# A gated block with a mixture of experts: when the second expert's down weights are loaded, and in which order the last step takes its chunks

## The reference, cut to what matters

```python
logits = x @ gate_w.T; scores = softmax(logits); topk_w, topk_idx = top_k(scores, 2)
buf = zeros((16, 256, 512)).at[sorted_e, pos].set(x[sorted_t])     # up to 256 tokens per expert
g = silu(buf @ w_gate[e]); u = buf @ w_up[e]                       # 512 -> 352
expert_out = (g * u) @ w_down[e]                                   # 352 -> 512
y = (gathered expert rows * topk_w).sum over the two experts
sh = (silu(x @ ws_gate) * (x @ ws_up)) @ ws_down                   # shared, 512 -> 704 -> 512
x = x + tanh(g_ffn) * (y + sh)                                     # x in the layer is normalised
```

## Time and profile before

| | before |
|---|---|
| median of 3 runs | 579.65 us (579.65 to 580.83) |
| profiled execution, its own time | 581.87 us |
| its span | 579.8 us |
| mean granted clock of TensorE | 0.985 |
| PE busy | 546.2 us (94%) |
| DVE busy | 419.4 us (72%) |
| ACT busy | 331.0 us (57%) |
| POOL busy | 154.3 us (27%) |
| moved between HBM and the core | 89.52 MB in all |

### The profile page before, as it was taken

The page is one execution under the profiler, slowest core; times in us unless marked ns, Lnnn a source line. Parts: engine busy times, 40 slices in busy tenths (PEclk is TensorE's granted clock), DMA queues, the critical chain, the costliest instruction groups (busy, mean ns, idle before and its releaser), DMA issues.

```text
span 579.8 us, 10175 instructions
## 1 busy us (share of the span) xinstructions
PE 546.2 (94%) x3768; PEld 464.0 (80%) x3776; DVE 419.4 (72%) x828; ACT 331.0 (57%) x570; POOL 154.3 (27%) x187
## 2 busy tenths in 40 slices
PE   7897879999999999999799999999999999999995
PEld 3453548986888788887799999999999999999983
DVE  3778988998899786586376666766676776566766
ACT  3285876686558527522367677766666666742321
POOL 3437780431043010104022211111111100166610
PEclk9988999999999999999899999999999999999998
DMA  7930130014001130115757776666777767457742
GB/s 265 386 131 2 37 136 11 2 37 145 1 5 35 73 101 1 77 46 165 244 165 263 246 252 222 222 222 227 242 244 260 245 218 241 148 167 214 232 147 99
DMA packets 45891, 89.52 MB, mean 154 GB/s; under 512 B 4304, under 2 KB 24784, under 8 KB 44832
## 3 DMA queue, kind: packets, MB, share of 16 engines
q1 hardware_dynamic: 40736, 72.26, 36.7%
q0 software_dynamic: 5120, 16.78, 9.3%
HBM read 72.25 MB, written 16.78 MB: 154 GB/s over the span
## 4 chain that ended last, share of the span: by engine, by line
PE 62%; DVE 19%; ACT 6%; POOL 6%; issue 4%; DMA 2%; another core or an unknown queue 1%; SPq 0%; DVEq 0%; POOLq 0%; ACTq 0%
PE ps_gu L1854 10%; PE ps_gu L1855 10%; PE ps_gu L1856 10%; PE ps_d L1854 6%; PE ps_d L1856 5%; PE ps_d L1855 5%; PE ps_a L2108 3%; PE ps_gu L1896 2%; POOL w L486 2%; DMA raw_d<-in_L_ffn_w_down 2%; PE ps_gu L2415 2%; POOL sw_lo L502 1%; PE ps_d L1875 1%; DVE bn_b L1093 1%; ACT y L754 1%
## 5 line engine op out<-in xcount | busy, mean ns | idle before, releaser
L1854 PE MATMUL ps_gu<-ex_xhi,w_hi 128*128 128x256 f32 x352 | 99.4, 283 | 0.2 <-DVE ex_xlo L1469 0.2
L1855 PE MATMUL ps_gu<-ex_xlo,w_hi 128*128 128x256 f32 x352 | 99.5, 283 | 0.0
L1856 PE MATMUL ps_gu<-ex_xhi,w_lo 128*128 128x256 f32 x352 | 99.4, 282 | 0.0
L1854 PEld LDWEIGHTS ps_gu<-ex_xhi,w_hi 128*128 128x128 f32 x352 | 67.0, 190 | 2.5 <-DVE ex_xlo L1469 0.5
L1855 PEld LDWEIGHTS ps_gu<-ex_xlo,w_hi 128*128 128x128 f32 x352 | 67.1, 191 | 1.8
L1856 PEld LDWEIGHTS ps_gu<-ex_xhi,w_lo 128*128 128x128 f32 x352 | 67.1, 191 | 0.0
L1854 PE MATMUL ps_gu<-xt_hi,sw_hi 128*128 128x256 f32 x220 | 65.1, 296 | 0.1
L996 ACT ACTIVATE ex_hhi<-ex_hid 128x256 fp32r<-128x256 f32 (+1 forms) x66 | 27.5, 417 | 64.6 <-DVE ex_hid L1715 58.0
L1855 PE MATMUL ps_gu<-xt_lo,sw_hi 128*128 128x256 f32 x220 | 62.0, 282 | 0.0
L1856 PE MATMUL ps_gu<-xt_hi,sw_lo 128*128 128x256 f32 x220 | 62.0, 282 | 0.0
L1854 PE MATMUL ps_d<-wd_hi,ex_hhi 128*128 128x512 f32 x132 | 54.3, 411 | 6.6 <-DVE ex_hlo L1717 6.5
(11 more groups left out here) (255 smaller groups left out, 1411.4 us busy)
## 6 DMA issues: line engine op xcount, KB each, us to landing
raw_gu<-in_L_ffn_w_gate SPq DMA_DIRECT2D x16, 704.0 KB
raw_gu<-in_L_ffn_w_up SPq DMA_DIRECT2D x16, 704.0 KB
raw_d<-in_L_ffn_w_down SPq DMA_DIRECT2D x16, 512.0 KB
expert_out_scratch<-eo SPq DMA_DIRECT2D x16, 512.0 KB
w<-in_fside_BxS2xS SPq DMA_DIRECT2D x4, 1024.0 KB, 5.4
x2n_scratch<-y SPq DMA_DIRECT2D x4, 1024.0 KB, 3.9
x<-in_x SPq DMA_DIRECT2D x1, 3072.0 KB, 16.5
raw_d<-in_L_ffn_w_down SPq DMA_DIRECT2D x16, 192.0 KB
```

The lines of the kernel that those rows point to most:

```text
L1854: pe.matmul(dst, a_hi, b_hi, start=start, stop=False)
L1855: pe.matmul(dst, a_hi, b_lo, start=False, stop=False)
L1856: return pe.matmul(dst, a_lo, b_hi, start=False, stop=stop)
```

## The change

There are three edits. SP loads expert 1's gate and up first, waits for them (32), and then issues the two down transfers; `weights_gu(1)` on ACT waits for 32, and `weights_d(1)` gets a wait for 64. In the last step the chunks are taken in the order 0, 2, 1 (`part_at`), on PE, ACT and DVE alike. On DVE, `add_rows` and `add_last` stand one slot of `hidden` earlier, and `last_rows` adds the first bank after a count of its own (`first_half_done`, raised by the third of the last six products) and the second after all of them.

```diff
+    def part_at(e, m):
+        return (0, 2, 1)[m] if e == NE - 1 else m
...
             sp.wait_ge(sh_gu, CHUNKS)
-            load_raw(1, 1)
+            load_gu(1, wg_v[1], wu_v[1])
+            sp.wait_ge(raw_in[1], 32)
+            load_d(1, w_down[1])
...
             def weights_gu(e, k, q):
-                act.wait_ge(raw_in[q], 32 if isinstance(e, int) and e == 0 else 64 * k + 64)
+                act.wait_ge(raw_in[q], 32 if isinstance(e, int) and e < 2 else 64 * k + 64)
...
             def weights_d(e, q):
+                if isinstance(e, int) and e < 2:
+                    act.wait_ge(raw_in[q], 64)
                 if isinstance(e, int) and e == 0:
-                    act.wait_ge(raw_in[q], 64)
                     emptied_b(act, unit_b(B - 1, B_LGT))
...
-            def hidden(e, q, m, first):
-                n, k = M * e + m, ROWS[m]
+            def hidden(e, q, m, first, part=None):
+                part = m if part is None else part
+                n, k = M * e + m, ROWS[part]
...
                 if not first:
-                    act.wait_ge(ex_d, n - M + 1)
-                act.activation(ex_hhi[0:k, m, :], ex_hid[0:k, (q + m) % 2, :], ACT.Copy).then_inc(ex_hi, 1)
+                    act.wait_ge(ex_d, n - m + part - M + 1)
+                act.activation(ex_hhi[0:k, part, :], ex_hid[0:k, (q + m) % 2, :], ACT.Copy).then_inc(ex_hi, 1)
...
             def last_rows():
-                dve.wait_ge(ex_d, M * NE)
                 dve.wait_ge(sum_last, HALF)
                 for k in range(HALF):
                     j = HALF * h + k
+                    if k == 0:
+                        dve.wait_ge(first_half_done, 1)
+                    else:
+                        dve.wait_ge(ex_d, M * NE)
...
             shared_rows(1)
-            hidden(E + 4, 0, 1)
             dve.wait_ge(ex_eo, E + 1)
             add_rows(2, 0)
+            hidden(E + 4, 0, 1)
+            add_rows(2, 1)
             hidden(E + 4, 0, 2)
-            add_rows(2, 1)
-            hidden(E + 5, 1, 0)
             dve.wait_ge(ex_eo, E + 2)
             add_last(0)
+            add_last(1)
+            hidden(E + 5, 1, 0)
+            add_last(2)
             hidden(E + 5, 1, 1)
-            add_last(1)
+            add_last(3)
             hidden(E + 5, 1, 2)
-            add_last(2)
-            add_last(3)
             last_rows()
...
-            def fill_d(q, bank, k, m, first, final):
+            def fill_d(q, bank, k, m, first, final, halves=None):
                 for h in range(HALF):
...
+                    if halves is not None and h == 0:
+                        last.then_inc(halves, 1)
                 last.then_inc(ex_d, 1)
```

More of the change, by code:

```diff
@@ L274, in flamingo_block @@
             sem(n) for n in ("ex_gu", "ex_sg", "ex_h", "ex_hi", "ex_lo", "ex_d", "ex_eo"))
-        cols_staged = sem("cols_staged")
+        cols_staged, first_half_done = sem("cols_staged"), sem("first_half_done")
         slot_cols, got_in, sum_half, sum_last, summed, out_done = (
@@ L988, in hidden @@
                 act.wait_ge(ex_gu, n + 1)
-                if m == M - 1:
+                if part == M - 1:
                     act.activation(ex_up[FOLDED:REST, :], ps_gu[REST:P, (q + m) % 2, 0:CAP], ACT.Copy)
@@ L1040, in _ @@
                 hidden(e, e % 2, 0, False)
-                hidden(e, e % 2, 1, False)
+                hidden(e, e % 2, 1, False, part_at(e, 1))
                 if e % 2 and t < len(TAIL):
                     tokens(E + t, t % 2)
-                hidden(e, e % 2, 2, False)
+                hidden(e, e % 2, 2, False, part_at(e, 2))
         @block.vector
@@ L1707, in hidden @@
             def hidden(e, q, m):
-                n, k = M * e + m, ROWS[m]
+                part = part_at(e, m) if isinstance(e, int) else m
+                n, k = M * e + m, ROWS[part]
                 dve.wait_ge(ex_sg, n + 1)
                 up = ps_gu[0:k, (q + m) % 2, CAP:2 * CAP]
-                if m == M - 1:
+                if part == M - 1:
                     dve.tensor_tensor(ex_up[0:FOLDED, :], ex_up[0:FOLDED, :], up[0:FOLDED], ALU.add).then_inc(ex_added, 1)
@@ L1716, in hidden @@
                 dve.wait_ge(ex_hi, n + 1)
-                dve.tensor_tensor(ex_hlo[0:k, m, :], ex_hid[0:k, (q + m) % 2, :], ex_hhi[0:k, m, :].bitcast(F32),
+                dve.tensor_tensor(ex_hlo[0:k, part, :], ex_hid[0:k, (q + m) % 2, :], ex_hhi[0:k, part, :].bitcast(F32),
                                   ALU.subtract).then_inc(ex_lo, 1)
@@ L2442, in tail_up @@
             def tail_up(t, w, m):
-                n, k = M * (E + 2 * t + w) + m, ROWS[m]
+                n, part = M * (E + 2 * t + w) + m, part_at(E + 2 * t + w, m)
                 if m == 0:
@@ L2449, in tail_up @@
                 pe.wait_ge(ex_h, n - 1)
-                fill_gu(n, (w + m) % 2, w, t % 2, k, m)
+                fill_gu(n, (w + m) % 2, w, t % 2, ROWS[part], part)
             def tail_down(t, w, m):
-                n, k = M * (E + 2 * t + w) + m, ROWS[m]
+                n, part = M * (E + 2 * t + w) + m, part_at(E + 2 * t + w, m)
+                final = m == M - 1 and w == 1
                 pe.wait_ge(ex_lo, n + 1)
@@ L2459, in tail_down @@
                     pe.wait_ge(ex_wdlo, E + w + 1)
-                fill_d(w, t % 2, k, m, m == 0 and w == 0, m == M - 1 and w == 1)
+                fill_d(w, t % 2, ROWS[part], part, m == 0 and w == 0, final, first_half_done if final and t == len(TAIL) - 1 else None)
             def step(e, k, q, first=False, evicted=True):
```

## The result

| | before | after |
|---|---|---|
| median | 579.65 us (578.91 to 580.83, 4 runs) | 572.19 us (571.55 to 574.51, 4 runs) |
| ratio, with its 95% interval | | 0.9879 [0.9857, 0.99] |
| profiled execution, its span | 581.87, 579.8 us | 572.15, 570.1 us |
| mean granted clock | 0.985 | 0.997 |

A forecast was written before the change was run, and what follows sets the result against it. PE is busy 94% of the span, so only its stalls, or work after it at the end, can give time back. Loads 4.7 plus tail 2.75 make 7.45 us off 579.65: 572.2 us, range 570.3 to 575.5.

The forecast's parts named there:

- The landing: Expert 1's gate and up land at 276.5, so expert 0's first down product starts at 281.0: 3.45 us gained.
- The clock: After PE's shortened gap before expert 0's down products, the clock stays at 1.00 instead of 0.66 for 5.0 us.
- DVE behind it: DVE's last weight part limits PE's start of expert 1, at restart + 6.4 (287.4 instead of 292.20): adds 1.3 us.
- Load 2: Expert 2's load, issued at 281, ends at 288.8 or 290.2; ACT wants it at 290.0; loads worth 4.7 us.
- The tail: End of the kernel: packed chunk second, DVE additions earlier and final additions split by bank, 2.75 us gained.
- DVE gives it at 565.3: Last step: `ex_hlo` of the first chunk is ready at 565.3, behind two `add_last`; 0.4 us lost to DVE.
- The baseline: Whole kernel: the gain, summed on the profiled execution of 581.87 us, is taken off the median of 579.65 us.
- (A): Expert 1's load: the count of 32 comes late with the gather, so the loads give nothing; 576.9 us, chance 0.07.
- (B): Expert 2's load is late, down weights landing at 284.3; the loads' gain shrinks to 1.5 us; 575.4 us, chance 0.06.
- (D): Slower: expert 1's down weights queue behind the gather and hold expert 2's load, ACT and PE; 581.3 us, chance 0.03.
- (C): ACT's unnamed wait moves into the last step and cancels the gain at the end; 575.0 us, chance 0.07.
- (E): The change doesn't do what it says, e.g. DVE's final wait still covers all products: +0.7, 572.9 us, within the forecast.

The follow-up runs named there:

- the control: The changed kernel run once more with no edit, in the second session: median 583.73 us, lowest 573.51.
- the reordered front: Changed kernel with ACT's first hidden chunk of expert 0 right behind `w_hi`, DVE's low weight parts of expert 1 before its tokens: median 584.47 us not applicable; 586.66 us, ratio 0.9923.
- the loads alone: Kernel before with only the edit of expert 1's loads and ACT's waits of 32 and 64: 574.78 us, ratio 0.9928.
- first session: Four kernels: only the loads edit, only the tail edits, chunks in order 0, 1, 2, old DVE order: 574.78, 577.0, 573.69, 573.0 us.
- third session: Changed kernel with both additions after all products, later row additions, front reordered, or three edits together: 584.47, 584.53, 586.66, 584.71 us; kernel before 581.58 to 602.27.

## Why the prediction was right, and where its terms were off

The forecast was 572.2 us for a median of 572.19, and its range and sign hold. That closeness is better than its terms deserve: the trace and the runs of single parts give 6.3 us where the sum had 7.45.

**The landing.** *"I take 276.5 as the landing"*, 7.76 us after the issue; measured 8.11 (8.02 to 8.31 in the nine executions). The packets were read rightly, the count was not. The load's packets after, by quarters: 274.25 to 274.5, then the load queue alone in the next quarter:

```profile
DMA packets 28, 0.07 MB, mean 297 GB/s; under 512 B 4, under 2 KB 13, under 8 KB 28
...
q1 hardware_dynamic: 1, 0.00, 0.2%
```

The last data packet (1408 bytes, between 512 B and 2 KB) lies in the first quarter, 7.3 to 7.6 us after the issue, as before (7.3 to 7.5), a last small one in the second, and ACT starts at 275.04. So the count reaches ACT 0.5 to 0.8 us behind the last data packet, where the sum had 0.25 to 0.5. The down product comes 12.63 after the issue instead of 12.26, and this term is 3.11 us instead of 3.45.

**The clock** stayed at 1.00, as taken. **DVE behind it** was the limit, as taken: PE begins expert 1 at restart + 6.77 instead of + 6.4, behind `wb`, the last weight part (restart is PE's first down product after its stop). The term is 1.0 us (restart to expert 2's transposes 16.40 before, 15.38 after) instead of 1.3. Together 4.13 for 4.7.

**Load 2** was held to be just in time, and it is only about that. Expert 2's gate was issued 12.82 after expert 1's (predicted 12.3), ACT wants it at restart + 9.12 (predicted + 9.0), and in the profiled execution names no wait. But of the eight executions with the new loads and an unchanged front three have ACT wait for it, 0.15 us in the control, 0.15 with the old DVE order and 0.52 in the first run with both additions after all products. Where ACT waits, the load arrives 8.95 to 9.79 us after its own issue, not the 7.8 of the sum. So there was no reserve, and this is why the reordered front stops at 0.6.

**The tail** is the term that was mis-sized: 2.75 in the forecast, 2.14 measured. Its parts, restart and end after the restart, tell where. From restart to end the text had 4.36 before and 2.5 after; measured 4.36 and 2.48. That PE could restart 1.26 earlier with DVE out of the way was right too: with the old DVE order it is 1.22 (31.03 in the loads alone, 29.81 with the changed chunks). The failing step is *"DVE gives it at 565.3"*, which gave DVE's delay as 0.4; it is 0.96. The text had the missing half in a conditional of its own: *"If that idle time is absent in other executions, DVE delays the chunk until 554.6 and PE by about 0.4"*. It is absent in after and in all four runs of the first session, so both delays apply: the down products of the two packed chunks show them, 0.49 us at step 20 and another 0.48 in the last step. The sum should have had them both.

**The baseline.** That conditional failed because the sum was made on an execution that carried ACT's unnamed wait (1.57 us of its end) and kept it on both sides: while ACT stood, DVE's moved additions looked covered. Taking the gain off the median rather than off this execution was right, since 574.4 would have been 2.2 too much. Whether the median of before itself holds some such waits, which would explain 7.0 to 7.46 where the parts give 6.3, isn't shown; the interval of the ratio allows either. So the hit at 572.2 is luck in part: the terms were 1.2 us too large by the traces, and the medians moved by 1.2 us more than the traces' parts.

**The rivals.** (A), the count that comes late with the gather: refuted. By the packets of after, the gather queue goes on for 0.5 to 0.7 us behind the count. 275 to 276, the only queue in it, and the quarter in which its data end:

```profile
q0 software_dynamic: 71, 0.21, 58.4%
...
q0 software_dynamic: 23, 0.06, 62.6%
```

ACT started at 275.04; the last of these data packets lies in 275.5 to 275.75. With the gather held until the load had landed the count came at 7.93 instead of 8.02 to 8.31, and just as far behind its last data packet, which lies between 273.25 and 273.5 there, with ACT starting at 274.02:

```profile
DMA packets 16, 0.01 MB, mean 56 GB/s; under 512 B 6, under 2 KB 16, under 8 KB 16
```

So the 0.5 to 0.8 us are not the gather's. The Trainium skill, DMA: Bandwidth & Descriptors, section on queues, rings and completion order, has an increment land behind every earlier write of the same engine, across its queues. The trace doesn't contradict that, since the gather's packets behind the count may be later writes; what it refutes is the reading by which the count waits for the whole gather. (B) and (D) needed the down weights to be late: SP saw them at 279.75 or before, 4.72 us after their issue. Of (B), load 2 being late, the 0.15 to 0.52 us of three executions are all that came. (C) did not occur in any last step. (E): no, each edit is worth something, 4.13, 0.91, 0.85 and 0.70 us (the last three taken out one at a time; together they are 2.14).

## What to carry to other kernels

When a consumer's wait covers more transfers than it reads, split the count first; whether the later transfers are issued at once or held back made only 0.1 to 0.4 us here. When additions are moved ahead of a chain that ends last, price both sides, what they take from the end and what they put into the chain, on an execution in which the chain is undisturbed: here 1.81 and 0.96 us. A profile that holds a wait with no named releaser is a poor baseline for a sum; look for the same stretch in a second execution before building on it.

## What was not expected of the hardware

ACT stands, with no releaser that the profile can name, for 1.9 to 9.5 us at a time, always at the first instruction of a hidden chunk, the one that waits for PE's count, but at another chunk in each execution, and only between 505 and 555 us, which is where POOL's gather of the expert rows runs (its issues go from 498.73 to 547.84 in after, and from 504.73 to 553.72 in before). In the first session's four profiles and in after there is none; in the nine others (before and the eight later ones) there are one to four. Control, then two of the third session (the reordered front and the additions after all products):

```profile
528.38 0.38 ACT L998 ACTIVATE ex_up<-ps_gu 32x256 f32<-32x256 f32 x1 [4.54 <-remote]
```

```profile
535.53 0.38 ACT L1000 ACTIVATE ex_up<-ps_gu 32x256 f32<-32x256 f32 x1 [8.79 <-remote]
```

```profile
533.11 0.38 ACT L998 ACTIVATE ex_up<-ps_gu 32x256 f32<-32x256 f32 x1 [6.66 <-remote]
```

For the last one the table by stretches shows what it costs (columns as in the first such table):

```profile
528.00:533.00 5.00, 4.67 (x25) 4.00 (x24) 1.64 (x3) 0.00 (x0) 3.05 (x4) 0.74 0.74 230
533.00:538.00 5.00, 2.60 (x14) 2.08 (x13) 3.15 (x6) 1.82 (x5) 1.32 (x2) 0.94 0.63 175
538.00:543.00 5.00, 5.00 (x30) 4.83 (x29) 4.48 (x9) 0.80 (x2) 3.27 (x3) 0.72 0.53 179
543.00:548.00 5.00, 5.00 (x37) 4.61 (x36) 1.85 (x3) 1.56 (x3) 2.87 (x4) 1.00 0.86 265
```

PE stands 2.7 us in the first two, and the granted clock, a mix of 2.4 and 1.2 GHz, is below 1.00 in three of them: about 5 x (0.26 + 0.06 + 0.28) = 3.0 us more. Together 5.7 us of the 9.4 by which the middle of that execution, 248.42 us, is longer than 239.0. Over all executions the middle goes with the waits that lie in it: 239.0 to 239.1 us in the five without any, 240.7 in the two whose waits there sum to 4.5 and 5.8, and 247.7 to 251.4 in the six with 6.6 or more. The one exception is before, with 239.08 beside a wait of 2.64. They stand in the kernel before and in changed ones alike, so they are not of the change. What releases them stays open: the traces show the gather and the waits in the same 50 us, but no run without the gather was made, so that it is their cause is not shown.
